# Reordering one tile's attention work on TensorE, ScalarE and VectorE in a two-block attention and expert kernel

## The reference

```python
# block 0: 128 keys for each window of 128 queries; block 1: 256 keys for each 256 queries
scores = jnp.einsum('bnqhd,bnkhd->bnhqk', qp, kp) * scale        # 16 heads of 16 numbers
attn = jax.nn.softmax(scores, axis=-1)
out = jnp.einsum('bnhqk,bnkhd->bnqhd', attn, vp).reshape(B, L, D)
return out @ out_w.T + out_b
...
x = x + _L0_xattn_ref(_layernorm(x, axis=-1), ctx_1024, ctx_1024, ...)
x = x + _L0_ffn_ref(_layernorm(x, axis=-1), ...)
x = x + _L1_xattn_ref(_layernorm(x, axis=-1), ctx_1024, ...)
x = x + _L1_ffn_ref(_layernorm(x, axis=-1), ...)
```

## Time and profile before

| | us |
|---|---|
| median of 3 executions | 1073.47 |
| lowest and highest | 1064.76, 1074.34 |
| the profiled execution's own time | 1076.29 |
| its span, first to last instruction | 1074.6 |

### The profile page before, as it was taken

How to read it: one execution, slowest core, us unless ns; L and a number is a source line. 1 busy time by engine, 2 the same in 40 slices (tenths; PEclk the granted TensorE clock), 3 DMA queues, 4 the chain that set the end, 5 groups by cost and what they waited for, 6 DMA issues and landing times.

```text
span 1074.6 us, 23613 instructions
## 1 busy us (share of the span) xinstructions
PE 794.8 (74%) x8366; PEld 599.1 (56%) x8367; DVE 595.4 (55%) x1396; ACT 372.2 (35%) x735; POOL 232.2 (22%) x248
## 2 busy tenths in 40 slices
PE   3968996587968999827969999650029999999900
PEld 1535653543637888714526666450029999899800
DVE  1546775347434777637666887469325445545513
ACT  2214554132222332311225666434224444444400
POOL 2100111003841222176100000004731101100065
PEclk9986998588989999969957999755559999999965
DMA  5992222372742333249950000446722233223234
GB/s 178 124 135 41 74 71 93 129 254 93 241 155 69 104 103 106 88 125 165 123 61 2 3 2 3 163 159 225 271 76 66 67 69 74 68 65 75 61 108 132
DMA packets 83804, 113.40 MB, mean 106 GB/s; under 512 B 16512, under 2 KB 64512, under 8 KB 83744
## 3 DMA queue, kind: packets, MB, share of 16 engines
q1 hardware_dynamic: 69712, 76.72, 28.3%
q0 software_dynamic: 12112, 34.49, 10.8%
q10 hardware_dynamic: 1920, 1.34, 0.4%
HBM read 65.19 MB, written 28.18 MB: 87 GB/s over the span
## 4 chain that ended last, share of the span: by engine, by line
PE 57%; DVE 15%; POOL 11%; issue 7%; DMA 5%; ACT 2%; SPq 1%; ACTq 0%; DVEq 0%; POOLq 0%
PE bank L725 16%; PE bank L738 12%; POOL slot_in L1361 7%; PE bank L533 5%; PE bank L554 3%; POOL arena L1382 3%; PE bank L502 3%; PE bank L710 2%; DVE neg_max L1067 2%; PE bank L463 2%; PE bank L474 2%; PE bank L520 2%; DMA arena<-in_ctxT 2%; DVE stats L1004 2%; DVE xn_buf L1014 2%
## 5 line engine op out<-in xcount | busy, mean ns | idle before, releaser
L725 PE MATMUL bank<-arena 128*128 128x128 f16 x3024 | 302.6, 220 | 3.4 <-DVE arena L1240 3.4
L738 PE MATMUL bank<-arena 128*128 x1224 | 281.1, 273 | 3.7 <-DVE arena L1248 2.0
L725 PEld LDWEIGHTS bank<-arena 128*128 x3024 | 264.5, 98 | 19.7 <-issue 4.1
L1361 POOL DMA_INDIRECT slot_in<-arena,slot x64 | 81.8, 1278 | 303.3 <-DVE slot L1208 284.3
L1067 DVE TENSOR_REDUCE neg_max<-bank 128x2 f32<-128x512 f32 (+1 forms) x192 | 125.0, 685 | 29.4 <-PE bank L502 28.1
L972 ACT ACTIVATE arena<-bank,arena 128x128 f32<-128x128 f32 x312 | 85.4, 381 | 123.9 <-DMA arena<-in_exp_b 107.9
L738 PEld LDWEIGHTS bank<-arena 128*128 128x128 f16 x1224 | 119.4, 98 | 12.1 <-issue 11.3
L1369 POOL DMA_DIRECT2D arena<-slot_in x87 | 47.9, 551 | 291.7 <-PE bank L710 273.7
L855 ACT ACTIVATE arena<-bank 128x1024 f32<-128x1024 f32 x96 | 96.5, 1026 | 11.2 <-PE bank L520 10.8
L710 PE MATMUL bank<-consts,arena 128*128 128x128 f32 x174 | 35.1, 286 | 74.9 <-DVE arena L1235 68.7
L502 PE MATMUL bank<-arena 48*128 48x128 f16 (+1 forms) x512 | 69.7, 271 | 11.8 <-DVE bank L1105 7.6
(11 more groups left out here) (126 smaller groups left out, 1089.9 us busy)
## 6 DMA issues: line engine op xcount, KB each, us to landing
arena<-arena SPq DMA_DIRECT2D x96, 128.0 KB, 6.7
arena<-slot_in POOLq DMA_DIRECT2D x87, 128.0 KB, 2.4
slot_out<-arena SPq DMA_DIRECT2D x87, 128.0 KB, 1.7
arena<-in_exp_up SPq DMA_DIRECT2D x16, 512.0 KB, 4.1
slot_in<-arena POOLq DMA_DIRECT2D x16, 384.0 KB, 2.9
arena<-in_exp_up SPq DMA_DIRECT2D x5, 1024.0 KB, 7.8
arena<-in_exp_dn SPq DMA_DIRECT2D x5, 1024.0 KB, 8.3
arena<-in_exp_b SPq DMA_DIRECT2D x39, 128.0 KB, 3.4
```

What stands on the lines that cost most here:

```text
L725: last = mm(upP[u][:, m // (UB // 2), m % (UB // 2) * P:(m % (UB // 2) + 1) * P], weights(e, 0, w, k * UPW[l] + m * P, P), rowsT[u][x][:, ...
L738: last = mm(yP[u], hidT[u][x][:, k], weights(e, 1, w, k * D, D), start=n == 0, stop=n == n_second - 1)
L1361: pool.indirect_dma_start(slot_in, bass.IndirectOffsetOnAxis(ap=slot[:, i, t:t + 1], axis=0), xn_all[l][:, t], None).then_inc(s["scattered ...
```

## The change

The order of one step is written anew for TensorE. The scores' first piece now stands ahead of `turn_maxima`. `turn_back` stands behind both and behind the first piece or pieces of maxima. `turn_attention` stands behind the first half of `values` instead of among the scores, `project_out` behind it and all remaining maxima. On ScalarE the copy for `turn_attention` comes behind the last exponential instead of the last but one (in block 0 these are the same place). On VectorE the divide comes behind `SPREAD[l][1]` reductions, which is now one in both blocks (it was one and two), then all other reductions, and the add last.

```diff
@@ -54,7 +54,7 @@
     NS = [48, 39]
     QUAD = 4
 
-    SPREAD = [[0, 1, 3, 4, 4], [0, 2, 3, 4, 5, 7, 8]]
+    SPREAD = [[0, 1, 2, 4], [0, 1, 3, 5, 6, 8]]
     GROUPS = NC
     SH = 512
     SHB = SH // P
@@ -555,24 +555,28 @@
                     last.then_inc(s["op_mm"], 1)
 
                 def step(i, u):
-                    first, left = isinstance(i, int) and i == 0, T - 1 - i if isinstance(i, int) else T
+                    first, left = i == 0, T - 1 - i
+                    ahead = SPREAD[l]
+
+                    def more(n):
+                        if left > 1:
+                            maxima(i + 2, ahead[n], ahead[n + 1])
+
+                    scores(i, 0)
                     if left > 0:
                         turn_maxima(i + 1, 1 - u)
-                    for p in range(NP):
+                    more(0)
+                    if not first:
+                        turn_back(i - 1)
+                    for p in range(1, NP):
                         scores(i, p)
-                        if left > 1:
-                            maxima(i + 2, SPREAD[l][p], SPREAD[l][p + 1])
-                        if p == 0 and not first:
-                            turn_back(i - 1)
-                        if p == max(NP - 2, 1) and not first:
-                            turn_attention(i - 1)
+                        more(p)
                     values(i, u, 0)
-                    if left > 1:
-                        maxima(i + 2, SPREAD[l][NP], SPREAD[l][NP + 1])
+                    if not first:
+                        turn_attention(i - 1)
+                    more(NP)
                     if not first:
                         project_out(i - 1)
-                    if left > 1:
-                        maxima(i + 2, SPREAD[l][NP + 1], NM)
                     values(i, u, 1)
 
                 pe.wait_ge(s["xT_ready"], NC)
@@ -853,7 +857,7 @@
                             after(act, s["pv_mm"], 2 * (i - 1) + half + 1)
                             dst = probs[p]
                         fn(dst.rearrange("p (b w) -> p b w", b=2), sc[p % 2], ACT.Exp, scale=SCALE / AS ** 2).then_inc(s["exp_done"], 1)
-                        if p == max(NP - 2, 1) and not first:
+                        if p == NP - 1 and not first:
                             copy_attention(i - 1)
                     act.wait_ge(s["pv_mm"], 2 * (i + 1))
                     after(act, s["ott_mm"], i)
@@ -1095,11 +1099,9 @@
                     if not first:
                         divide(i - 1)
                     if left > 1:
-                        maxima(i + 2, u, SPREAD[l][1], SPREAD[l][2 * KW + 1])
+                        maxima(i + 2, u, SPREAD[l][1], NM)
                     if not first:
                         add(i - 1)
-                    if left > 1:
-                        maxima(i + 2, u, SPREAD[l][2 * KW + 1], NM)
 
                 dve.wait_ge(s["qparts_ready"], NC)
                 v.memset(attP, 0.0).then_inc(s["v_ready"], 1)
```

## The result

The changed kernel takes 1128.34 us (median of 4, 1120.48 to 1134.21) against 1071.99 us before (median of 4 here): ratio 1.0533, interval 1.0443 to 1.0623. The forecast was 1090 with a range of 1078 to 1106. The direction was right and the size was not: +56 us where +16.4 was worked out.

A forecast was written before the change was run, and what follows sets the result against it. TensorE bounds block 1's attention, VectorE next. Block 1's 14.6 + 0.4 + 2 - 0.6 = +16.4 us, block 0's 0, on the profiled 1076.29 give 1092.7; against a median 2.8 less, 1090 us, range 1078 to 1106.

The forecast's parts named there:

- Items 1 to 6, the chain: Block 1's waits between turns of maxima: 8.77 us a full-clock tile instead of 7.54, +14.6 us over 12 tiles.
- The low-clock tile: Block 1's tile at half clock: loss between 0 and 1.2 us, taken as 0.4.
- the first tile: Block 1's first tile has no divide and saves up to 0.6 us.
- Block 0: Old waits go, new ones come: -0.04 us a tile, taken as 0 in all, bounds -3 to +3 us.
- Rival (c): Gaps in block 1 delay or drop the clock: 1095 to 1099 for one or two tiles, 1140 for all twelve; chance 0.12.
- the tail: Block 1's last two tiles, without maxima: late turn of attention and copy, 0.9 to 1.2 us each, +2 for both.
- The argument against it: Against a clock fall in block 1: block 0 kept full clock with its waits of 0.16 and 0.24 us.
- Its sign of being wrong: Forecast wrong if block 1's clock stays low past the second tile, or maxima piece 3 starts without a wait.
- The rule on modes: Changing tiling mode drains TensorE; 10 changes a tile instead of 11 would alone gain an estimated 0.1 us a tile.
- The rule on the clock: Short idle times between groups of matmuls let the clock swing between two levels; no row at full clock showed it.
- Rival (a): VectorE's chain does not hold TensorE, only removed waits and cheaper maxima pieces count: 1061 us; chance 0.06.
- Rival (b): TensorE and VectorE take the loss back in part: a block 1 tile at +0.5 us, +8, 1081 us; chance 0.13.

The follow-up runs named there:

- two-pieces run: Changed kernel with two VectorE reductions ahead of block 1's divide and two maxima pieces ahead of the turn back, against the kernel before: ratio 1.0116.

## Why the prediction was right and wrong, point by point

**Items 1 to 6, the chain: right.** Each start is within 0.1 us, and the full-clock tile has a mean of 8.79 for 8.77. TensorE stands for 1.19 us of the tile shown, where the sum had 1.6. Twelve tiles at 8.77 - 7.54 are 14.8 us, not 14.6, which changes nothing. The run with the wait filled isolates this term: +14.3 us where +16.4 had been worked out. The earlier divide alone (+5.6) shows that the second reduction behind the divide is what holds piece 3.

**The low-clock tile: too small.** I took 0.4 us, with an end at 1.2. The tile at half clock from 563.22 to 576.79 took 13.57 against 12.63, +0.9. Against it, the first tile took 9.83 for 10.92, -1.1 where the sum had -0.6. That hardly counts, but the low tile was the number that every fall of the clock would be priced with: 13.6, not 13.0.

**Block 0: right.** The sum had 0, the run with block 0 alone has 1.0011, and the last add moved by 0.1 us. By the tile it is +0.04 us (5.38 and 5.57 in turn for 5.39 and 5.48) and not -0.04, as the copy holds the projection for longer than the 0.1 us that was given to it.

**The step that failed: the clock taken as unchanged.** The forecast priced twelve tiles at full clock, +14.6 us, and its sum had nothing for a fall of the clock. Rival (c) named the swing and the places, with 1095 to 1099 for one or two tiles and 1140 for all twelve, and got 0.12. The mean clocks of all 4 executions were low (0.81 to 0.82 for 0.853), and in the profiled one the swing cost 36.1 us in the twelve tiles and a part of the tail's 5.9: with the wait filled and the clock high, the tail grew by 1.7 us (693.3 to 712.1), which is the +2 of the sum, so some 4 of the 5.9 are the clock too. That this swing comes from TensorE's standing is shown by three runs: filling the wait ends it, the same work elsewhere does not, and a longer wait in the old order brings it.

The argument against it was that block 0 kept its clock with its waits, but those were 0.24 and 0.16 us, 0.4 and 0.5 us of a tile in all, and the new ones 0.26, 0.72 and 0.21, 1.19 in all. The longest new wait, three times the old one, was judged by the old; the prediction had worked out the 1.6 us of standing itself and did not carry it to the clock. Its sign of being wrong, low clock past the second tile, did not fit either: the kernel before already rises only after its third tile, and what mattered was a fall after the rise.

**The rule on modes: no run here tells it apart.** The chain was priced from spacings that hold the changes of mode already, so its 8.77 against the measured 8.79 says nothing about one change fewer.

**The rule on the clock.** The Trainium skill's case of short idle times between groups of matmuls (TensorE: Matmul & The Clock Gate, A second HAM failure mode) is what the trace after shows: idle times of 0.21 to 0.72 us between groups of products, and stretches at 1.00 and 0.50 in turn. It deserved a greater chance than 0.12.

**Rival (a)** is excluded: piece 3 waits for 0.72 us. **Rival (b)** is too, since VectorE's pace kept pieces 4 and 5 at 0.60 us each and the full-clock tile is 1.25 us longer, not 0.5.

What stays open is how the clock decides. Full-clock tiles with 0.72 us of waiting at piece 3 alone held it, and so did 0.7 to 0.8 us at piece 4 in the profiled execution of the two-pieces run, whose tile is only 0.3 us shorter than the changed kernel's. TensorE stood for 0.76 and 0.85 us of such a tile in all, in the changed kernel for 1.19. Where between these the swing begins, and why the changed kernel at times stays low for three tiles and at times for one, the runs don't tell.

## What to carry to other kernels

When a change leaves TensorE standing in each turn of a loop, price two things: the time it stands, from the spacing of rows, and what the loop costs if it runs in part at half clock; here the first was 15.0 us and the second 36.1. A queue in program order passes a delay on: one reduction moved behind a divide held the next matmuls, since two banks were all that lay between the engines. And when a stage swings, a look at the granted clock by stretch settles in one view what the spans can't.

## What the runs showed of the hardware

Useless work can pay: eight products in a wait took the ratio from about 1.04 to 1.014, and the same eight products some 2 us later in the tile took nothing off that could be seen (1.049). In this loop level and load follow each other: at half clock the products fill VectorE's chain (6.70 us busy of 6.70), the clock rises, the gaps open (11.12 of 13.40), and it falls. That the gaps bring the fall is tested by the runs above. What brings the rise is not: in the stretch from 634.80 PE was busy for 33.12 of 33.90 us, and the clock stayed low all that time.

The same kernel before had medians of 1090 us on two chips and 1072 us on a third, 1.7% apart, more than most effects here. Times taken across the chips would have hidden the +0.3%, +0.7% and -0.5% above. What differs between the chips, the runs don't tell.
